# One hand-written order of steps replaced by another in a decoder layer on one core

## The reference, cut to what matters

```python
x = layernorm(x + attn(x))         # linear attention, 16 heads: exp features, K'V, denominator, Wproj
x = layernorm(x + xattn(x, ctx))   # softmax attention to ctx, 16 heads of 8
h = gelu(x @ ternary(W_fc).T)      # 128 -> 512
h = layernorm(h) * ln_w + ln_b
x = layernorm(x + h @ ternary(W_proj).T)
```

## Time and profile before

| | |
|---|---|
| median of 3 runs | 619.97 us (619.82 to 620.43) |
| the profiled execution's own time | 619.85 us |
| its span, first to last instruction | 617.4 us |
| mean granted TensorE clock | 0.987 |
| busy: PE, DVE, ACT, POOL | 591.3, 479.2, 464.6, 487.3 us |

### The profile page before, as it was taken

The page is one execution under the profiler, slowest core; times in us unless marked ns, Lnnn a source line. Parts: engine busy times, 40 slices in busy tenths (PEclk is TensorE's granted clock), DMA queues, the critical chain, the costliest instruction groups (busy, mean ns, idle before and its releaser), DMA issues.

```text
span 617.4 us, 31077 instructions
## 1 busy us (share of the span) xinstructions
PE 591.3 (96%) x13344; PEld 433.7 (70%) x13344; DVE 479.2 (78%) x1235; ACT 464.6 (75%) x875; POOL 487.3 (79%) x653
## 2 busy tenths in 40 slices
PE   9999999999999999999999999999999999997684
PEld 6686767777677867767686867767686857665554
DVE  2555677887888887888878887888878887988676
ACT  3636566978878797878879787878879787959563
POOL 5065144798989998898989999999988989998845
PEclk9999999999999999999999999999999999999699
DMA  8113222353544536363554646363644636254501
GB/s 337 72 37 114 64 80 72 79 142 73 132 87 123 115 107 130 76 161 73 134 94 131 116 100 136 70 168 73 134 88 135 118 79 123 63 124 78 98 18 53
DMA packets 116154, 64.89 MB, mean 105 GB/s; under 512 B 94321, under 2 KB 100850, under 8 KB 115890
## 3 DMA queue, kind: packets, MB, share of 16 engines
q1 hardware_dynamic: 116018, 62.91, 42.9%
HBM read 17.27 MB, written 4.19 MB: 35 GB/s over the span
## 4 chain that ended last, share of the span: by engine, by line
PE 71%; POOL 14%; ACT 5%; issue 4%; DMA 4%; DVE 2%; SPq 1%; POOLq 0%; ACTq 0%; DVEq 0%
PE bank L337 15%; PE bank L327 8%; PE bank L357 8%; PE bank L449 4%; POOL gall L1185 3%; ACT PT L665 3%; POOL gs L1190 2%; PE bank L318 2%; PE bank L435 2%; PE bank L414 2%; PE bank L276 2%; PE bank L492 2%; PE bank L278 2%; PE bank L277 2%; DMA pack<-Mrow 2%
## 5 line engine op out<-in xcount | busy, mean ns | idle before, releaser
L337 PE MATMUL bank<-Mh,GT 128*32 128x128 f32 x4096 | 128.6, 274 | 0.0
L337 PEld LDWEIGHTS bank<-Mh,GT 128*32 128x32 f32 x4096 | 107.1, 110 | 18.5 <-issue 14.3
L918 DVE TENSOR_REDUCE mx<-bank 128x8 f32<-128x512 f32 x128 | 79.0, 682 | 16.3 <-PE bank L414 16.2
L665 ACT ACTIVATE PT<-bank 128x512 f32<-128x512 f32 x128 | 64.4, 625 | 16.8 <-PE bank L435 16.8
L550 ACT ACTIVATE GT<-bank 128x512 f32<-128x512 f32 x95 | 51.8, 596 | 29.4 <-PE bank L327 26.9
L1185 POOL TENSOR_TENSOR gall<-gall,lnr 128x512 f32<-128x512 f32 x56 | 73.2, 1310 | 0.5 <-DVE st L853 0.5
L1190 POOL TENSOR_TENSOR gs<-gall,gs 128x512 f16<-128x512 f32 x56 | 64.9, 1161 | 9.5 <-ACT gs L702 9.4
L550 ACT ACTIVATE Cb<-bank 128x512 f32<-128x512 f32 x66 | 39.0, 594 | 43.7 <-PE bank L357 29.4
L327 PE MATMUL bank<-kp,xs 64*128 64x512 f32 x256 | 70.6, 627 | 0.0
L1132 POOL TENSOR_TENSOR rstd<-ve,mhalf 128x4 f32<-128x4 f32 x60 | 61.3, 1022 | 5.0
L357 PE MATMUL bank<-Cb,qT 128*64 128x128 f32 x1024 | 59.4, 274 | 0.0
(11 more groups left out here) (203 smaller groups left out, 1524.9 us busy)
## 6 DMA issues: line engine op xcount, KB each, us to landing
pack<-Qh SPq DMA_DIRECT2D x64, 128.0 KB, 2.6
xT<-in_xT SPq DMA_DIRECT2D x16, 256.0 KB, 3.0
xs<-in_x_nat SPq DMA_DIRECT2D x16, 256.0 KB, 3.0
cxT<-in_cxT SPq DMA_DIRECT2D x16, 256.0 KB, 3.0
Kp<-Kh SPq DMA_DIRECT2D x32, 128.0 KB, 2.1
pack<-Ql SPq DMA_DIRECT2D x32, 128.0 KB, 2.9
out_y<-yo SPq DMA_DIRECT2D x15, 256.0 KB, 2.4
Kp<-Kl SPq DMA_DIRECT2D x16, 128.0 KB, 2.1
```

What stands on the lines that cost most here:

```text
L337: m = e.matmul(bk[32 * j:32 * j + 32, tile(g_)], GT[b % 4][:, tile(hh, 32)], Mh[:, tile(hh)], start=True, stop=True)
L665: e.activation(PT[tp][:, tile(j, 512)], bank[uses["prob", s, i][0]][:, :], ACT.Exp, scale=SM).then_inc(emptied("prob", s, i)[0], 1)
L918: e.tensor_reduce(to, bank[uses["score", s, i][0]][:, :].rearrange("p (g b k) -> p g b k", g=2, b=4), AX.X, ALU.max).then_inc(emptied("sco ...
```

## The change

The three texts are replaced; nothing else is. Both lists hold the same 1325 pairs of step and batch. What differs is the order, and on which engine some copies and norms are done: in the period ap3 loses its plus (11 batches' third norm goes to VectorE; the tail keeps it on ScalarE for four), c3 gains one (16 batches), and some twelve single copies of the head and the tail change sides. In the period the four up steps follow one another behind down2 and down3. down0 goes ahead of rows, and rows ahead of gl2. c1, ks, c2 and pv0 stand at the end of a period in place of the start of the next, and so does qpack. ab2, split, loadc and loadx are moved too. In the tail the stats of the first half of the second norm (st2h0) and of batch 14's g (stat) go ahead of oturn1.

```diff
--- before.py
+++ after.py
@@ -33,25 +33,25 @@
 HEAD = """
-wk wb wq k0 k1 k2 WkT g0 zeros g1 g2+ mh0 split small1 mh1 g3+ k3 q0 c0+ c1+ WqT split@1 loadx Wvp ks c2 Wff c3 xw loadx@1 kst g4+ g5 g6+ small2 g7+
-q1 k0@1 q2 q3 gam g0+@1 bv g1+@1 k1@1 c4+ c5+ dT nbeta qz loadc k2@1 bias3 bias2 bc c6 c7+ biasA o g2+@1 xb csplit loadx@2 st1 g3@1 kproj k3@1 ap1+
-loadc@1 x1s csplit@1 sbar vproj c0@1 kpack loadc@2
+wk zeros split wq WkT small1 wb k0 k1 k2 WqT k3 g0 g1+ mh0 g2+ g3 mh1 xw q0 loadx ks kst Wvp c0 c1+ c2 c3+ small2 g4 g5 g6+ loadc g7+ bv k0@1 q1 q2
+nbeta gam csplit c4+ c5+ g0+@1 split@1 g1@1 q3 k1@1 bias2 c6+ dT c7 xb k2@1 biasA bc bias3 loadx@1 qz o Wff g2+@1 loadc@1 st1 g3+@1 k3@1 x1s csplit@1
+kproj c0+@1 ap1+ ks@1 c1@1 c2@1 loadx@2 vproj sbar kpack qpack split@2
 """
 PERIOD = """
-split@-1 c1 c2 ks pv0@2 g4 g5 up0@3 down2@4 up1@3 gs0@3 down3@4 up2@3 up3@3 q0 stat@3 c3 cs0@2 kst ab1@1 pv1@2 oturn0@2 q1 gs1@3 q2 qproj@1 q3 gh0@3
-qpack@1 c4 ap3+@5 oturn1@2 c5+ dT g6+ g7+ kproj k0@-1 cs1@2 kpack gl0@3 vproj proj0@2 k1@-1 gl1@3 k2@-1 score0@1 gs2@3 gh1@3 loadx@-2 c6+ c7+ score1@1
-xb g0+@-1 g1+@-1 g2+@-1 gs3@3 gh2@3 g3+@-1 proj1@2 gl2@3 k3@-1 st2@2 rows@1 gl3@3 gh3@3 csplit@-1 bc c0+@-1 ap2+@2 o prob0@1 st1 prob1@1 down0@3 st3@4
-x1s loadc@-2 ab2@2 down1@3 ap1+
+g4 g5 down2@4 down3@4 kst gs0@3 ab2@3 up0@3 up1@3 up2@3 up3@3 stat@3 q0 q1 c3+ c4 cs0@2 pv1@2 oturn0@2 loadc@-1 ab1@1 qproj@1 q2 kpack q3 kproj vproj
+gh0@3 c5+ dT gl0@3 oturn1@2 g6+ g7+ k0@-1 cs1@2 k1@-1 k2@-1 gs1@3 proj0@2 score0@1 c6+ c7+ gh1@3 score1@1 gs2@3 gl1@3 g0+@-1 g1+@-1 g2+@-1 g3+@-1
+proj1@2 xb gs3@3 loadx@-2 k3@-1 st2@2 down0@3 rows@1 gh2@3 gl2@3 bc gh3@3 gl3@3 c0+@-1 st3@4 ap2+@2 o st1 csplit@-1 x1s split@-2 prob0@1 prob1@1 ap3@4
+down1@3 qpack c1@-1 ap1+ ks@-1 c2@-1 pv0@1
 """
 TAIL = """
-down2@5 c1@1 ks@1 pv0@3 pv1@3 cs0@3 up0@4 cs1@3 gs0@4 tw@1 up1@4 up2@4 oturn0@3 qpack@2 oturn1@3 kpack@1 g4+@1 ap3+@6 c2+@1 down3@5 stat@4 gs1@4 up3@4
-kproj@1 qproj@2 c3@1 proj0@3 kst@1 q0@1 c4+@1 proj1@3 gh0@4 q1@1 g5+@1 g6@1 gs2@4 gl0@4 q2@1 g7+@1 q3@1 st2@3 score0@2 c5+@1 dT@1 gl1@4 score1@2 gh1@4
-gh2@4 c6+@1 c7+@1 xb@1 gs3@4 bc@1 rows@2 gl2@4 o@1 ap2+@3 gl3@4 gh3@4 st1h0@1 prob0@2 down0@4 st1h1@1 st3@5 prob1@2 ap1h0+@1 ap1h1+@1 down1@4 down2@4
-ab2@3 pv0@2 ab1@2 oturn0@2 pv1@2 up0@3 gs0@3 down3@4 up1@3 flip@1 qpack@1 gs1@3 stat@3 up2@3 up3@3 gl0@3 qproj@1 oturn1@2 vproj@1 proj0@2 ap3+@5
-proj1@2 gl1@3 st2@2 gh0@3 gh1@3 gs2@3 score0@1 score1@1 ap2+@2 gh2@3 down0@3 rows@1 gs3@3 gh3@3 flip3@2 gl2@3 down1@3 gl3@3 ab2@2 prob0@1 ab1@1
-prob1@1 st3@4 down2@3 pv0@1 up0@2 oturn0@1 down3@3 pv1@1 proj0@1 up1@2 ap3+@4 oturn1@1 up2@2 st2h0@1 up3@2 ap2h0+@1 proj1@1 st2h1@1 turn0+@2 turn1+@2
-st3@3 ap2h1+@1 stat@2 flip3h0@1 turn2+@2 turn3@2 flip3h1@1 down0@2 up0@1 ab2h0@1 down1@2 up1@1 ab2h1@1 up2@1 down2@2 up3@1 ap3+@3 down3@2 turn0+@1
-st3@2 turn1+@1 stath0@1 stath1@1 down0@1 down1@1 turn2+@1 turn3+@1 ap3+@2 down2@1 st3h0@1 down3@1 st3h1@1 ap3h0@1 ap3h1@1
+ab2@4 cs0@3 oturn0@3 q0@1 up0@4 gs0@4 down2@5 c3+@1 up1@4 gs1@4 down3@5 stat@4 kst@1 up2@4 cs1@3 up3@4 q1@1 pv1@3 qproj@2 gs2@4 g4+@1 gl0@4 g5+@1
+oturn1@3 q2@1 q3@1 g6+@1 kproj@1 proj0@3 gl1@4 xb@1 dT@1 gh0@4 gh1@4 c4@1 proj1@3 score0@2 c5+@1 score1@2 g7+@1 gh2@4 gs3@4 gl2@4 st2@3 c6+@1 c7+@1
+rows@2 kpack@1 bc@1 gl3@4 gh3@4 ap2+@3 o@1 st1h0@1 prob0@2 down0@4 st1h1@1 ab2@3 st3@5 down1@4 ab1@2 gs0@3 gs1@3 prob1@2 down2@4 pv0@2 ap1h0+@1
+ap1h1+@1 down3@4 oturn0@2 up0@3 pv1@2 up1@3 up2@3 qpack@1 flip@1 stat@3 up3@3 qproj@1 gh0@3 gh1@3 gl0@3 oturn1@2 proj0@2 gl1@3 proj1@2 st2@2 ap3+@5
+vproj@1 gs2@3 gs3@3 score0@1 score1@1 ap2+@2 gh2@3 flip3@2 down0@3 ab2@2 gh3@3 rows@1 gl2@3 up0@2 gl3@3 down1@3 prob0@1 prob1@1 ab1@1 st3@4 turn0@2
+down2@3 pv0@1 oturn0@1 up1@2 down3@3 up2@2 pv1@1 up3@2 ap2h0+@1 proj0@1 ap3+@4 st2h0@1 tw@1 turn1+@2 stat@2 oturn1@1 turn2+@2 flip3h0@1 st3@3 down0@2
+proj1@1 up0@1 turn3+@2 ap3+@3 ap2h1+@1 st2h1@1 down1@2 ab2h0@1 down2@2 down3@2 up1@1 st3@2 stath0@1 turn0+@1 flip3h1@1 turn1@1 down0@1 up2@1 stath1@1
+ab2h1@1 up3@1 turn2+@1 ap3+@2 down1@1 turn3+@1 down2@1 st3h0@1 down3@1 st3h1@1 ap3h0@1 ap3h1@1
 """
```

## The result

The changed kernel takes 622.26 us (median of 9 runs, 620.18 to 626.42), the kernel before 619.82 us on the same chip (9 runs, 617.74 to 620.43): ratio 1.005, 95% interval 1.0032 to 1.0068. It is slower by 2.4 us by the medians; the ratio, which is not their quotient (1.0039), stands for 3.1 us. 1.9 us faster was forecast, and 622.26 lies outside the range given (615.0 to 621.4). The profiled execution of after happened to be the slowest of its nine (626.42 us, span 624.6), so some 4 us of what it shows over before (span 617.4) are not in the median; the other eight spans lie between 618.4 and 623.1 us. One profiled execution further on, of the new periods with the old tail, took 680 us at a granted clock of 0.85; no reading uses it.

A forecast was written before the change was run, and what follows sets the result against it. TensorE was taken as the bound, busy 591.3 of 617.4 us, with the idle time in the end. Terms +0.3 -1.2 +0.3 -0.2 -1.0 = -1.8 us gave 618.1 us; range 615.0 to 621.4.

The forecast's parts named there:

- Boundaries of kinds: Places in TensorE's order where kinds of matmul meet, about 0.1 us each: +0.02 us a period, +0.3 in all.
- Mrow: SyncE's queue: the row of maxima goes ahead of gl2, so three excess waits of TensorE go: -1.2 us.
- qpack: Moved to its period's end: 0.24 us less TensorE work covers Ql, score0 waits in two or three periods: +0.3 us.
- x1T: c4 ahead of qproj in place of q2 gives 0.24 us more cover for one 1.1 us wait: -0.2 us.
- down0: Moved ahead of rows, 7 us earlier, with 2 us left for gT0: cost nothing, up to 2 us a period.
- The head: Start of the run: TensorE never idles from 9 us on, nothing to win: 0, bounds 0 and +1.5 us.
- Third norm: 11 batches move from ScalarE to VectorE, which gains 1.2 us a period; no cost, GpSimd slowing taken as 0.
- Rival A: GpSimd becomes the bound of the period, 35.6 us against 34.7 if no wait shrinks: +1.8, 621.8 us; chance 0.20.
- Tail: The last batch's chain after the last o ends 1.0 us earlier: -1.0, bounds -4 and +3 us.
- First half: Tail: flip comes with no down3 before it; qproj, score0 and prob come 0.4 to 0.5 us earlier.
- Statistics: Tail: the first half's come ahead of oturn1, 1.2 us earlier; those of stat(14) some 4 us earlier.
- Second half: Tail: last batch's up2 some 4 us later, last rstd of the fourth norm 0.3 earlier; bound +3 us.

The follow-up runs named there:

- twin of before: The kernel before with each of its 85 transposing transfers replaced by two plain copies of half the size: 618.9 us, ratio 0.9972.
- twin of after: The changed kernel with the same plain copies in place of transposing transfers: 623.3 us, ratio 1.0046 to the kernel before.
- second trace of the twin: The twin of after run once more, unchanged, as control on another chip: ratio 1.0031 to the kernel before.
- exchanged tail: Two kernels with plain copies: changed head and periods with the old tail, ratio 0.9996; old head and periods with the changed tail, 1.0005.
- cover edit: The twin of after with c4 and q2 changing places in the period, giving TensorE 8.95 us of work between qproj and score0: ratio 1.0095.

## Why the prediction was wrong

The step that failed is the tail, put at -1.0 us and measured at +2 to +3. The qpack term was sized too small beside it. The terms one by one:

- **Boundaries of kinds, +0.3: right.** Quiet periods are 34.69 us in the twin of before and 34.70 to 34.71 in that of after. Splitting two blocks cost 0.12 us a boundary, where I had 0.1.
- **Mrow, -1.2: right.** Its waits left the periods, and the twin of before, which has none of them, is 1.2 us shorter between the marks. That the two figures agree to a tenth is in part luck: the third excess was added without a row, and profiles of equal periods differ by 0.5.
- **qpack, +0.3: right mechanism, wrong size.** The waits of score0 are 1.6 and 1.7 us in the traces of after and its twin, and 0.9 in the second trace of the twin. Between the marks the new periods cost 1.7 us in the twins, 1.2 on average over eight profiles, and 1.5 or 2.5 by the exchanged tail. I had taken the landing of Ql from before as fixed, and only the cover as changed. The landing changed too, since the step moved against the instruction transfers, and both are needed: the old periods have late landings and no wait, the cover edit 8 late ones and one wait. My own far bound of 0.24 us in every period had room for it.
- **x1T, -0.2: nothing,** 1.1 us before, 1.2 after. **down0: nothing,** as said. **The head, 0: not told apart:** the first mark comes 0.36 us later in after and 0.2 in its twin, but kernels with one and the same head spread by 1 us and more there.
- **Third norm, 0: right, with its own figure off.** It runs at L896, another line than I named, and takes 1.8 to 2.0 us a period where I had 1.2, since its first instruction is held until GpSimd's L1171 is done. Moving it back changed nothing. Rival A did not happen, and the slowing that it counted on runs the other way for this norm.
- **Tail, -1.0: the step that failed,** measured +2.1 between the profiles of the twins, +2.0 and +3.1 by the two exchanges, and some +2.6 in the original pair (the estimate of 68 against 65.4). Its parts follow.
- *First half.* "flip comes with no down3 before it" was a misreading: down3(12) stands ahead of flip(15) in both lists. New there is up2(13), pv1(14) now stands behind up0(13), and vproj(15) behind proj1(14); flip came 1.0 us and prob0(15) 1.8 us later, not 0.5 earlier.
- *Statistics.* Those of the first half came 1.3 us later in the twins after the last o, since prob0(15) did; from prob0(15) on they gained 0.5 us, where I had 1.2 from that step. L1205, the end of stat(14), came 1.2 us earlier where I had 4 for its statistics, and VectorE's wait of 3.0 us for it fell to 0.5. The stretch from prob0(15) to down0(14) is 2.1 us shorter by all this.
- *Second half.* I put it 4 us late with the end unharmed: up2(15) was 7.3 us later after the last o, and the last stretch grew by 2.3 us.
- *Left out.* I counted nothing for the wait on x2T(13), 1.8 us in after and 1.2 in its twin, which comes since its statistics stand behind eight maxima on VectorE and, once these are out of the way, its transfer behind kpack and gl3 on SyncE; nor for the clock, which was lower in the tail of some executions than of others.

The rivals on the slow side named only GpSimd. The place that lost most was the one where my working was longest and rested least on rows.

## What to carry to other kernels

When steps are put in another order, add up the chain of the last batch step by step from the list itself, and count what stands ahead of each step of it, not only what is moved. Where the tail leaves TensorE idle, expect its clock to differ from one execution to the next (0.87 or 0.79 over the last 25 us here), and do not read a small gain or loss from one profile of it. And treat the landing time of a small transfer as a spread (here 2.5 to 4.3 us), not as the number it had in the old order; 0.24 us of cover decided here whether the long end cost anything.

## What the hardware showed that was not expected

- TensorE's own instructions come in by DMA, 106 pieces of 16 KB in this run, and when a piece starts between 0.3 us before and 1.55 us after the issue of a 128 KB transfer (Ql), this lands in 3.1 to 4.3 us in place of 2.5, in 115 of 115 cases.
- An instruction of VectorE that otherwise takes 0.33 to 0.36 us (L896) took 0.99 to 1.16 when it started beside GpSimd's L1171, and ended 0.08 us after it, in 11 of 11 periods; L1171 kept its 1.16 us.
- A wait of 1.8 us in the tail was followed by a product of 1.94 us that takes 1.10 at full clock, with a granted clock of 0.64. In nine other profiles with such a wait (1.0 to 1.8 us) the product took 1.10.
- The time of equal executions of a kernel spreads by 2 to 6 us, and part of that goes with the clock: in the twin of after, the five executions at a mean clock under 0.984 took 624.2 us on average, the other five 622.2. In the profiles the last 25 us run at half speed for 2 to 7 us, or for 10.
